# A lane of its own for the choice of experts, tensor operands in the normalising passes, and a new order, in a fused eight-sequence kernel on one core

## The reference, cut to what matters

```python
x = L0_attn_X_embed                                   # (8, 512, 128)
x = x + embed_attention(_layernorm(x), Wq, bq, ...)   # diag(softmax over axis 1 of QK/sqrt(512)) * V
x = x + local_ffn(_layernorm(x), ...)                 # 2 layers: window-64 attention, 8 heads of 64, rotary factors; gated FFN of 341
x = x + global_attention(_layernorm(x), ...)          # 16 heads of 8, causal over 512 rows
x = x + moe(_layernorm(x), ...)

# inside moe:
scores = softmax(x @ gate_w)                          # 8 experts
topk_w, topk_idx = top_k(scores, 2)
topk_w = topk_w / (sum(topk_w) + 1e-20)
for e in range(8):
    hid = silu(x @ w_gate[e]) * (x @ w_up[e])         # 128 -> 256
    y = y + w_per_expert[:, e:e + 1] * (hid @ w_down[e])
return y + silu(x @ ws_gate) * (x @ ws_up) @ ws_down  # the shared expert, the ninth
```

## Time and the profile before

| | |
|---|---|
| time, median of 3 runs | 1709.93 us (1705.53 to 1713.02) |
| the profiled execution | 1709.73 us, span 1708.0 us |
| granted TensorE clock, mean of the span | 0.977 |
| PE busy | 1532.9 us (90%) |
| DVE busy | 1233.1 us (72%) |
| ACT busy | 965.7 us (57%) |
| POOL busy | 600.9 us (35%) |
| DMA moved | 80.13 MB |

### The profile page before, as it was taken

One profiled execution on the slowest core, in us unless ns is written; L12 is line 12 of the kernel. 1 busy time (PEld: TensorE's weight loads), 2 busy tenths in 40 slices (PEclk: granted clock), 3 DMA queues, 4 the chain that ended last, 5 costly groups with the idle time before them and its releaser, 6 DMA issues.

```text
span 1708.0 us, 29745 instructions
## 1 busy us (share of the span) xinstructions
PE 1532.9 (90%) x11632; PEld 908.0 (53%) x11632; DVE 1233.1 (72%) x2636; ACT 965.7 (57%) x1786; POOL 600.9 (35%) x401
## 2 busy tenths in 40 slices
PE   5779987899998999888999999988998889988999
PEld 2444553545565555645556465554555445645556
DVE  5877878776688657985588856886669547885544
ACT  3475765456654766548745577448653553662451
POOL 1866836152071612625044430716106115110000
PEclk8999999899999999999999999999999999998999
DMA  4200000310160101601024100421016002504102
GB/s 140 68 2 22 23 7 22 75 24 1 44 135 17 24 10 52 124 10 24 19 67 108 25 2 29 112 54 24 11 37 140 3 1 69 118 3 106 46 10 69
DMA packets 37293, 80.13 MB, mean 47 GB/s; under 512 B 6783, under 2 KB 22655, under 8 KB 33777
## 3 DMA queue, kind: packets, MB, share of 16 engines
q1 hardware_dynamic: 37152, 78.22, 19.1%
HBM read 54.74 MB, written 8.78 MB: 37 GB/s over the span
## 4 chain that ended last, share of the span: by engine, by line
PE 30%; DVE 9%; ACT 8%; issue 2%; POOL 2%; POOLq 0%; DVEq 0%; ACTq 0%
PE ps L500 27%; DVE bsmall L1346 2%; ACT work L957 2%; PE ps L505 2%; ACT bigs L1040 2%; DVE fsmall L1219 1%; POOL work L1497 1%; DVE fsmall L1211 1%; ACT L1066 1%; POOL fsmall L1476 0%; DVE work L1182 0%; ACT bigs L1066 0%; ACT L1002 0%; POOL work L1508 0%; DVE x L1436 0%
## 5 line engine op out<-in xcount | busy, mean ns | idle before, releaser
L1476 POOL TENSOR_TENSOR fsmall<-fsmall,consts 128x8 f32<-128x8 f32 (+1 forms) x140 | 201.5, 1452 | 200.9 <-DVE fsmall L1115 193.2
L1497 POOL TENSOR_TENSOR work<-work 128x1024 f32<-128x1024 f32 x56 | 137.0, 2447 | 379.9 <-DVE work L1182 379.8
L500 PE MATMUL ps<-bxt,mw 128*128 128x512 f32 x504 | 251.1, 605 | 6.0 <-DVE bigs L1448 4.2
L500 PE MATMUL ps<-maskb,identb 128*128 128x128 bf16 (+1 forms) x1152 | 228.7, 239 | 19.3 <-ACT work L957 15.1
L957 ACT ACTIVATE work<-ps,fsmall 128x128 f32<-128x128 f32 x448 | 164.5, 510 | 44.0 <-DVE fsmall L1223 43.6
L1346 DVE TENSOR_REDUCE bsmall<-ps 128x1 f32<-128x512 f32 (+3 forms) x308 | 177.5, 632 | 14.6 <-PE ps L500 14.2
L1040 ACT ACTIVATE bigs<-ps 128x512 f32<-128x512 f32 x280 | 151.9, 652 | 29.7 <-PE ps L500 29.0
L500 PE MATMUL ps<-wqkv,h 128*128 128x512 f32 x336 | 159.5, 601 | 9.2 <-ACT vs L917 5.5
L505 PE MATMUL ps<-ident,work 128*128 128x128 f32 x924 | 133.5, 285 | 32.6 <-ACT work L957 15.6
L1528 POOL TENSOR_TENSOR work<-work,fsmall 128x1024 f32<-128x1024 f32 x56 | 106.1, 1896 | 150.9 <-DVE fsmall L1214 150.9
L1066 ACT ACTIVATE bigs<-ps 128x512 f32<-128x512 f32 x126 | 75.1, 597 | 139.1 <-PE ps L500 138.3
(11 more groups left out here) (337 smaller groups left out, 3005.8 us busy)
## 6 DMA issues: line engine op xcount, KB each, us to landing
mw<-in_experts SPq DMA_DIRECT2D x63, 384.0 KB, 3.2
pks<-scr_partsb SPq DMA_DIRECT2D x42, 192.0 KB
pqs<-scr_partsb SPq DMA_DIRECT2D x126, 64.0 KB
v2s<-vs SPq DMA_DIRECT2D x14, 512.0 KB, 4.4
v2s<-vs SPq DMA_DIRECT2D x14, 384.0 KB, 5.8
scr_partsb<-bigs SPq DMA_DIRECT2D x7, 768.0 KB, 3.7
wqkv<-in_experts SPq DMA_DIRECT2D x9, 384.0 KB, 3.1
out<-x SPq DMA_DIRECT2D x7, 256.0 KB, 12.0
```

Of the source, the lines that this page charges most:

```text
L500: return nc.tensor.matmul(o, a, b, start=start, stop=stop, skip_group_check=True)
L1476: return nc.gpsimd.tensor_tensor(out, x, consts[:, k:k + 1].broadcast_to([x.shape[0], x.shape[1]]), op)
L1497: nc.gpsimd.tensor_tensor(R.qk[:, m, :], R.qk[:, m, :], R.part[m % 2], ALU.add).then_inc(R.l_add.sem, 1)
```

## The change

It does six things:

1. `route` of `backs` becomes a fifth lane, R, with a chain of signals of its own. The products of the first experts may now stand ahead of the gate product in PE's stream, and the first `add_expert` waits for the gates (`r_w`) by name.
2. `normalise` uses `scalar_tensor_tensor`: the inverse deviation comes as a second tensor, one column repeated 128 times, instead of a second scalar.
3. The first embed of `fronts` uses four PSUM banks, as front0's does, and its waits between products fall away.
4. `scale_rotary` handles one layer per call. Layer 0 comes after front0's score maxima, layer 1 after its second `normalise`; readers wait for their layer.
5. SP waits for both before its first expert loads, and no longer waits for an expert's down product where it loads nothing after.
6. All five strings of `ORDER` are new.

The numbers of instructions stay: 7584 matmul and transpose instructions, 128 of DVE's `tensor_scalar` become `scalar_tensor_tensor`, and the same DMAs.

```diff
-        "BBEBEBEBEBEBEEEBBBBEBFFFFBFFBFFFFFFBFBFFFBBBFFBBBBBFFFFBFFFFBFFFFBBBFFFFFFBFBBFFBBFFBBFBFBFFFFBBBBBFFFFFBFBF"
+        "BBEBEEBBBEBEEEBBBEBBFFBFFFBFFBFBFFFFFFFFBFBFBBBFBBFBFFBFFFFBFFBFBFBBBBFFFFFFBBFBFFBFFBFBFFBBFFBFFBFBFBFFBFBF"
...
-        self.eb = [self.fb[3]] * 4 if beside else self.fb
...
+        self.br = sig("route_vector", 15, kind=Chain)
-        self.bv, self.b_var = sig("back_vector", 26, kind=Chain), sig("b_var_guarded", 2)
+        self.bv, self.b_var = sig("back_vector", 11, kind=Chain), sig("b_var_guarded", 2)
...
+        def on_one_bank(R, s):
+            return R.beside and s > 0
+        def embed_banks(R, s):
+            return [R.fb[3]] * 4 if on_one_bank(R, s) else R.fb
...
-                if R.beside:
+                if on_one_bank(R, s):
                     yield "kv"
                     pe.wait_ge(R.a_qk.sem, R.a_qk.at(s, 1))
...
-                    elif R.beside:
+                    elif on_one_bank(R, s):
                         pe.wait_ge(R.a_e.sem, R.a_e.at(s, b))
...
+                if R is back7:
+                    yield from route(R, s)
+                yield from experts(R, s)
+
+            def route(R, s):
                 yield "route"
...
                             yield f"moe{e}{c}" + "gu"[j]
+                            if e == 0 and c == 0 and j == 0:
+                                pe.wait_ge(R.b_xt.sem, R.b_xt.at(s, 2))
...
-            def scale_rotary():
+            def scale_rotary(l):
                 dve.wait_ge(loaded_rotary, 16 * len(rotary_loads))
-                for l in range(LAYERS):
...
                 i.then_inc(ready_r, 1)
-                dve.wait_ge(ready_r, 1)
...
-                    i = ts(xn[:, tt, :], src[:, tt, :], mv[:, tt, 0:1], rs[:, 1, tt:tt + 1], ALU.subtract, ALU.mult)
+                    i = stt(out=xn[:, tt, :], in0=src[:, tt, :], scalar=mv[:, tt, 0:1],
+                            in1=rs[:, 1, tt:tt + 1].broadcast_to([P, P]), op0=ALU.subtract, op1=ALU.mult)
...
-                if R is front0:
-                    scale_rotary()
...
+                if R is front0:
+                    yield "rotary0"
+                    scale_rotary(0)
...
+                if R is front0:
+                    yield "rotary1"
+                    scale_rotary(1)
...
                     dve.wait_ge(R.m_d.sem, R.m_d.at(s, e + 1))
+                    if e == 0:
+                        dve.wait_ge(R.r_w.sem, R.r_w.at(s, 1))
...
-            sp.wait_ge(ready_r, 1)
+            sp.wait_ge(ready_r, LAYERS)
...
-                    sp.wait_ge(R.m_d.sem, R.m_d.at(s, e))
                     if e + SLOTS - 1 < ALL or not last:
+                        sp.wait_ge(R.m_d.sem, R.m_d.at(s, e))
                         load_expert(R, (e - 1 + SLOTS) % ALL)
```

More of the change, by code:

```diff
@@ L112 @@
+        "BBFFFFFFFFBF"
     ),
@@ L156, in run_lanes, with all_lanes @@
         assert next(lane, None) is None
-def all_lanes(front, back, embed, enter, fronts, front0, backs, back7):
+def all_lanes(front, back, embed, enter, route, fronts, front0, backs, back7):
     def rounds(half, room):
@@ L163, in all_lanes @@
     return (chain(rounds(front, fronts), rounds(back, back7)), chain(rounds(front, front0), rounds(back, backs)),
-            rounds(embed, fronts), chain.from_iterable(enter(backs, s) for s in range(1, backs.count)))
+            rounds(embed, fronts), chain.from_iterable(enter(backs, s) for s in range(1, backs.count)),
+            rounds(route, backs))
 def is_first(s):
@@ L868, in experts @@
                 down(ALL - 1)
-            run_lanes(pe, ORDER["tensor"], *all_lanes(front, back, embed, enter, fronts, front0, backs, back7))
+            run_lanes(pe, ORDER["tensor"], *all_lanes(front, back, embed, enter, route, fronts, front0, backs, back7))
         @block.scalar
@@ L1066, in experts @@
                         nc.scalar.activation(R.silu[k % 3], R.bb[n % banks][:, :], ACT.Silu).then_inc(R.m_silu.sem, 1)
-            run_lanes(act, ORDER["scalar"], *all_lanes(front, back, embed, enter, fronts, front0, backs, back7))
+            run_lanes(act, ORDER["scalar"], *all_lanes(front, back, embed, enter, route, fronts, front0, backs, back7))
         @block.vector
@@ L1370, in back, with route @@
                 normalise(s, 2, R.x3, R.bxn, R.bmv, R.brs, R.b_rstd, R.b_xn)
+                finish(R.bv)
+                if R is back7:
+                    yield from route(R, s)
+                yield from experts(R, s)
+            def route(R, s):
+                R.br.start()
                 yield "route"
@@ L1453, in experts @@
                 add_expert(ALL - 1)
-            run_lanes(dve, ORDER["vector"], *all_lanes(front, back, embed, enter, fronts, front0, backs, back7))
+            run_lanes(dve, ORDER["vector"], *all_lanes(front, back, embed, enter, route, fronts, front0, backs, back7))
         @block.gpsimd
@@ L1557, in back, with route @@
                 rstd(s, 2, R.b_stats, R.bmv, R.brs, R.b_var, R.b_rstd)
-            run_lanes(pool, ORDER["gpsimd"], *all_lanes(front, back, embed, enter, fronts, front0, backs, back7))
+            def route(R, s):
+                yield from ()
+            run_lanes(pool, ORDER["gpsimd"], *all_lanes(front, back, embed, enter, route, fronts, front0, backs, back7))
         @block.sync
@@ L1652, in experts, with route @@
                 sp.dma_start(out[bass.ds(R.first + s, 1), :, :].rearrange("o (a p) e -> p (o a) e", p=P), R.outb[:, :, :]).then_inc(R.stored, 16)
-            run_lanes(sp, ORDER["sync"], *all_lanes(front, back, embed, enter, fronts, front0, backs, back7))
+            def route(R, s):
+                yield from ()
+            run_lanes(sp, ORDER["sync"], *all_lanes(front, back, embed, enter, route, fronts, front0, backs, back7))
             for R in (backs, back7):
```

207 lines of the change are left out of this document (103 added, 104 removed).

## The result

The changed kernel takes 1689.54 us (median of 4 runs, 1682.24 to 1693.07), the kernel before 1707.73 us (1704.68 to 1713.02, 4 runs): ratio 0.9881, 95% interval 0.9854 to 0.9907, so 1.2% faster: 18 us by the two medians, 20 by the ratio. The profiled execution took 1693.07 us, its span 1691.3, at a mean granted clock of 0.975.

The account below looks back on a forecast made before the run. It took four limits in turn: latency at the start, POOL, PE with gaps, DVE in one late stretch. 1709.7 + 0 − 2.5 + 0 − 2.6 − 1.7 = 1702.9, so 1703.0 us; range 1690 to 1714 (its own 1698 to 1708).

Parts of the forecast that it names:

- The normalising passes: DVE's 128 normalise instructions: the tensor operand is held under POOL's operations like the scalar one, so worth 0.
- rival A: In normalise, the tensor operand frees DVE from POOL's hold, giving 1697 us; chance 0.15.
- The start: First 50 us: moved rotary factors, maxima and second normalise let POOL's next operation start earlier; −2.5 us, ends −1 and −3.8.
- The choice of experts: In the backs, DVE's chain choosing experts was already covered by PE's work, so moving it is worth 0, ends ±3.
- The late stretch: From 1300 us, DVE-bound: PE gets more work before it must wait for DVE; −2.6 us, ends 0 and −4.3.
- My sign: For 1300 to 1350 us: PE busy over 41 of 50 us would show the predicted gain there.
- The other stages: Rest of the 14 layers: the new order fills the same frame, by two sums of PE shortfalls; −1.7 us, ends ±8.
- The bound: Whole kernel: PE busiest in every stretch, with limits taking turns: latency at the start, POOL, PE with gaps, late DVE.
- The signs: PE idle under 50 us in five local-attention stretches shows B; 400 to 1300 us changing over 8 us shows the prediction wrong.
- the five stretches: Windows with local attention beside the back's score passes, where PE idled 60.7 us in all before the change.
- B: Rival: the new order fills PE gaps in local-attention stretches that the sums miss, 15 us, giving 1688 us; chance 0.25.
- C: Rival at the start: one idle PE piece of about 6 us keeps the clock low, +16, 1719 us; chance 0.08.

Follow-up runs that it names:

- operand_alone: The kernel before with only the tensor operand put into normalise, nothing else changed: 1707.24 us against 1706.80, ratio 1.0009.
- old_to_290_then_new: The changed kernel's code in the old order up to the second front's local attention (about 288 us), new order from there: 1689.46 us against 1706.71, ratio 0.9900.

## Why the prediction was wrong, point by point

- **The normalising passes, 0.** Right. The row of L1310 decided well: two tensor operands are held under POOL, 3.22 us for a free 1.14, so the rule of the Trainium skill (GPSIMD Engine Reference, 1. Specifications) holds for this operand too, and rival A is refuted by two kernels. It says that POOL and VectorE contend for SBUF when an instruction of VectorE's has two inputs there. By the Trainium skill's VectorE: DVE Perf Modes, The perf-mode tier table, which gives `tensor_scalar` twice the rate of `tensor_tensor` in float32, I had estimated 8.5 us more of DVE. The trace has less: the free group takes 1.14 us against 1.11, and all 128 take 48.29 us in operand_alone against 46.96, 1.3 us more.
- **The start, −2.5 (−1 to −3.8).** Right in mechanism: POOL's powers come 3.25 us earlier where I had worked out 2.5, and the held group takes 1.13 us. The size is less sure: the kernel with this part alone is 3.6 us (0.9 to 6.5) faster than before, but with the new order behind it the same start showed no gain.
- **The choice of experts, 0 (±3).** Not a term by itself, and as one it was wrong. I took DVE's chain as covered at either place. The gate product on PE may indeed be moved back at no cost, but DVE's and ACT's steps at their new place cost 20 us in the old order, and at their old place 26 us in the new one.
- **The late stretch, −2.6 (0 to −4.3).** Within its ends, but not settled. My sign came about (PE busy 42.38 of 50 us, DVE no longer near 50). The stages from 1303 us to the end are 3.9 us shorter in old_to_290_then_new, in which the moved split is one change among many. The whole times don't show it: with and without the new order behind 1300 us they are 0.9881 and 0.9885.
- **The other stages, −1.7 (±8).** This step failed. My text said that the order "fills the same frame" since two sums of shortfalls came out alike. The stages from 701 to 1303 us alone gave 3.7 + 1.2 + 6.3 = 11.2 us, and the one at 289 us another 2.4. Neither sum held the waits that went: in the stage at 1100 us 3.0 us hung on two `normalise` groups held under POOL (3.89 and 2.68 us in before). I had these holds in the 11.4 us of excess, and asked only whether the operand would free them. That the new order might keep `normalise` clear of POOL elsewhere, as I saw it do at the start, I did not look up.
- **The sum** forecast 6.8 us and 18 to 20 came. It was short by 10 to 12 us in that one term (11.2 or 13.6 us measured against 1.7), and by about 1 us each in the start and the late stretch.
- **The bound.** I wrote that PE is the busiest engine in every stretch. The rows that I read beside it say otherwise for three: DVE 31.51 against PE's 29.37 in the first 50 us, POOL 49.23 against 34.83 in the next 50, DVE 46.76 against 39.33 from 1300 to 1350 us.
- **The signs.** Two of them would have misled. PE's idle time in the five stretches was 56.3 us, not under 50, though B's time came. And the stages from 499 to 1303 us are 5.6 us shorter in the changed kernel's trace (804.0 to 798.4), within the 8 us that I allowed, in part because its stage at 499 us ran at a clock of 0.97 (204.1 us against 198.5); in old_to_290_then_new they are 14.8 us shorter, 3.5 of them by the clock.
- **Rivals.** B, with 0.25, came true in time, and gaps were filled, as its reason says, in the stages from 701 us on. The lane alone gives none of it; whether the order needed the lane's freedom stays open. Its 15 us were a quarter of the idle time and not worked out from waits, so that the number fits is luck. C's premise, one idle piece of 6 us at the start, came about and did not lower the clock from 40 to 70 us.

What stays open: of the 6.3 us at 1100 us about 3.3, the 3.7 us at 701 us, the 2.4 at 289 us and the gain behind 1303 us are not traced to single waits; that they come from the order is shown, by which rows is not.

## What to carry to other kernels

A relaid order can't be priced by two of its chains: list every wait over half a microsecond in one full stage of before, and look up for each what stands in its place after. A hold of one engine by another is lifted by an operand only if a row shows it; a new order did lift it in the three groups where I moved a step for that alone: find the long operations of POOL and see which DVE passes lie beside them before and after. And cut long kernels at a landmark and join the halves of two versions; stage lengths at equal clock repeat to 0.3 us where whole times scatter by 10.
